# Decoder layer, cross-attention: the last slot of a pair of heads issues no value product, the first slot of the next pair issues two

## The reference

```python
q = (x @ Wq).reshape(B, S, 8, 64); k = (context @ Wk)...; v = (context @ Wv)...
attn = jnp.einsum('bhsd,bhld->bhsl', q, k) * 64 ** -0.5
attn = jax.nn.softmax(attn, axis=-1)
out = jnp.einsum('bhsl,bhld->bhsd', attn, v)
x = layernorm(x + out.reshape(B, S, 512) @ Wo + bo)
```

## Time and profile before

| | |
|---|---|
| median of 3 runs | 1456.46 us (1456.46 to 1459.16) |
| the profiled execution | 1461.65 us, its span 1459.9 us |
| mean granted TensorE clock | 0.906 |
| TensorE busy | 1227.4 us, 84% of the span |
| VectorE, ScalarE, GpSimd busy | 739.8, 579.5 and 683.9 us |
| the cross-attention's matmuls L1587 | 372.3 to 1089.7 us |

### The profile page before, as it was taken

One profiled execution on the slowest core, in us unless ns is written; L12 is line 12 of the kernel. 1 busy time (PEld: TensorE's weight loads), 2 busy tenths in 40 slices (PEclk: granted clock), 3 DMA queues, 4 the chain that ended last, 5 costly groups with the idle time before them and its releaser, 6 DMA issues.

```text
span 1459.9 us, 20289 instructions
## 1 busy us (share of the span) xinstructions
PE 1227.4 (84%) x6416; PEld 706.0 (48%) x6416; DVE 739.8 (51%) x1328; ACT 579.5 (40%) x999; POOL 683.9 (47%) x597
## 2 busy tenths in 40 slices
PE   4487787875899999999999999999994359999970
PEld 3255454543555555555545555555533336666640
DVE  6575858636335673456734667346613522222217
ACT  3365555642444554445544445444441012222210
POOL 0033333331357875578755877558782521111111
PEclk8688888975899999999999999999995579999995
DMA  5590000010000010000100000000004811111113
GB/s 176 177 303 16 1 1 0 0 46 23 0 1 1 1 46 1 1 1 1 46 2 1 1 1 24 0 1 1 1 1 138 293 56 44 42 46 45 45 51 136
DMA packets 33008, 64.66 MB, mean 44 GB/s; under 512 B 4222, under 2 KB 22399, under 8 KB 32641
## 3 DMA queue, kind: packets, MB, share of 16 engines
q1 hardware_dynamic: 23200, 32.41, 6.9%
q10 hardware_dynamic: 6304, 22.59, 4.9%
q0 software_dynamic: 3408, 8.43, 1.7%
HBM read 52.89 MB, written 28.34 MB: 56 GB/s over the span
## 4 chain that ended last, share of the span: by engine, by line
PE 68%; DVE 14%; issue 9%; ACT 4%; DMA 2%; POOL 1%; another core or an unknown queue 1%; ACTq 1%; SPq 0%; DVEq 0%; POOLq 0%
PE PS L1587 15%; PE PS L1598 11%; PE PS L1694 9%; PE PS L1515 9%; PE PS L1711 5%; PE PS L1528 3%; PE PS L1422 2%; PE PS L225 2%; DVE mxp L1173 2%; PE PS L1432 2%; PE PS L1411 2%; PE PS L226 2%; PE PS L227 2%; PE PS L1703 1%; PE PS L1568 1%
## 5 line engine op out<-in xcount | busy, mean ns | idle before, releaser
L609 POOL TENSOR_TENSOR acc<-acc,PX 128x1024 f32<-128x1024 f32 (+1 forms) x176 | 419.8, 2385 | 124.8 <-ACT PX L851 118.1
L851 ACT ACTIVATE PX<-PS 128x1024 f32<-128x1024 f32 (+1 forms) x208 | 213.3, 1025 | 266.5 <-PE PS L1587 262.3
L1173 DVE TENSOR_REDUCE mxp<-PS 128x2 f32<-128x804 f32 x256 | 241.6, 988 | 140.0 <-PE PS L1528 140.0
L1598 PE MATMUL PS<-PX,V 128*64 128x512 f32 (+1 forms) x832 | 223.3, 616 | 3.5 <-ACT O_raw L814 3.5
L551 POOL TENSOR_SCALAR_AFFINE_SELECT A<-A 128x128 f32<-128x128 f32 x256 | 89.1, 360 | 217.5 <-ACT A L752 214.0
L1694 PE MATMUL PS<-W,XBT 128*128 x312 | 148.8, 600 | 1.3 <-ACT XBT L907 1.3
L752 ACT ACTIVATE A<-PS 128x512 f32<-128x512 f32 (+3 forms) x256 | 99.4, 437 | 96.1 <-PE PS L1422 88.9
L670 POOL DMA_INDIRECT Y<-yb,goal_u x39 | 38.4, 985 | 201.0 <-DVE yb L1332 195.9
L1587 PEld LDWEIGHTS PS<-QH,KH 64*128 64x128 f32 (+1 forms) x416 | 38.3, 180 | 152.7 <-issue 89.5
L1422 PE MATMUL PS<-qT,kT 128*128 128x512 f32 (+3 forms) x256 | 87.4, 416 | 27.3 <-ACT A L752 22.0
L1587 PE MATMUL PS<-QH,KH 64*128 64x512 f32 (+1 forms) x416 | 104.0, 497 | 1.6 <-ACT MR L836 0.7
(11 more groups left out here) (261 smaller groups left out, 2068.9 us busy)
## 6 DMA issues: line engine op xcount, KB each, us to landing
W<-in_w SPq DMA_DIRECT2D x24, 512.0 KB
XB<-XG ACTq DMA_DIRECT2D x39, 129.0 KB, 2.1
yl<-Y SPq DMA_DIRECT2D x4, 1024.0 KB, 9.0
X<-in_x SPq DMA_DIRECT2D x1, 2048.0 KB, 12.1
out<-X SPq DMA_DIRECT2D x4, 512.0 KB, 2.9
xt_raw<-in_xt SPq DMA_DIRECT2D x3, 512.0 KB, 4.2
c_raw<-in_ctxt SPq DMA_DIRECT2D x6, 200.0 KB, 2.5
c_raw<-in_ctxt SPq DMA_DIRECT2D x12, 100.0 KB, 2.7
```

Of the source, the lines that this page charges most:

```text
L609: ins = pool.tensor_tensor(sums[0:r], sums[0:r], PX[0:r, (NL * p + t) % NP, :, :], ALU.add)
L851: act.activation(PX[0:r, u % NP, :, :], PS[0:r, score_buffer(u):score_buffer(u) + 2, :], ACT.Exp, scale=XD ** -0.5)\
L1173: dve.tensor_reduce(mxp[:, p % 2, :, v % NT, v // NT:v // NT + 1].rearrange("p a o -> p (a o)"), PS[:, k:k + 2, 0:BW], AX, ALU.max)\
L1598: mm = pe.matmul(PS[rows, 4, :], V[0:LROWS[j], j, P * p + XD * half:P * p + XD * half + XD], PX[0:LROWS[j], u % NP, half, :], start=(j == ...
```

## The change

TensorE's order of value products is changed at each boundary of two pairs. Before, the last slot (j = 12) of a pair issues the product of slot 11, and the first slot of the next pair that of slot 12. Now the last slot issues none, and the first slot of the next pair (or, from the fourth pair, of the next element) issues both, 11 and then 12. At the very end of the stage nothing moves: the products of slots 11 and 12 of the last pair stand behind the score products as before, only the first of them is now written behind the loop nest instead of in its last slot. The other slots, and the other engines, are as before. No wait is added or removed.

```diff
--- before.py
+++ after.py
@@ -1612,10 +1612,14 @@
                             scores_t(b + 1, 0)
                         for d, s in maxima(p, j, more) + early(p, j, first, more):
                             step(b + d, s)
-                        if u >= 1:
+                        if j == 0 and u >= 1:
+                            values_t(b, u - 2)
                             values_t(b, u - 1)
-                        elif not first:
+                        elif j == 0 and not first:
+                            values_t(b - 1, U - 2)
                             values_t(b - 1, U - 1)
+                        elif 1 <= j < NL - 1:
+                            values_t(b, u - 1)
                         for d, s in late(p, j, first, more):
                             step(b + d, s)
 
@@ -1626,6 +1630,7 @@
             with pe.Fori(1, B - 1) as b:
                 cross_attention(b, False, True)
             cross_attention(B - 1, False, False)
+            values_t(B - 1, U - 2)
             values_t(B - 1, U - 1)
             for s in EPILOGUE:
                 step(B - 1, s)
```

## The result

| | before | after |
|---|---|---|
| median of 22 runs each | 1458.62 us | 1454.03 us |
| lowest to highest | 1456.42 to 1462.46 us | 1448.82 to 1459.18 us |
| ratio of the medians, 95% interval | | 0.9966, 0.9953 to 0.9978 |
| the profiled execution, its span | 1461.65, 1459.9 us | 1454.91, 1453.2 us |
| first score product to the last totals ("stage") | 372.3 to 1097.1: 724.8 us | 369.5 to 1088.2: 718.7 us |

The change makes the kernel 0.34% faster: 4.6 us between the medians, where 5.0 us were forecast. The time itself, 1454.03, is 2.5 us above the forecast of 1451.5, mostly because the median of before over 22 runs is 2.2 us above that of the three runs from which the 5.0 were taken.

What follows compares the result with a forecast made beforehand. TensorE's own instruction stream was taken to bound the cross-attention stage. Boundary terms 3.06 + 0 + 1.22 + 0.71 = 5.0 us, taken off the median of 1456.46, gave 1451.5 us, range 1449.0 to 1456.6.

Steps and rivals of the forecast that it cites:

- Ordinary boundary: Nine pair boundaries without context preparation: same matmuls, fewer changes of kind, 0.19 from scores plus 0.15 from values, 0.34 us each.
- Rival 2: Neighbouring matmuls of one kind save nothing; only 1.5 us gained in all, median 1455.0 us; chance 10%.
- Nothing new waits there: At ordinary boundaries the reordered score, value and totals products meet no new wait on exponentials, QL or ACT's copies.
- O_raw boundaries: Pairs 2 to 3 of the first three elements: TensorE arrives 0.34 us earlier, waits that much longer; 0 us gained.
- Entry and exit of the loop: Two element crossings: the two value products side by side, the value projection's wait for QL gone; 0.61 us each.
- The way back: Taken branch of the element loop: less cover for its 3.43 us, but the value projection starts earlier; 0.7 us gained.
- The clock, zero net: Granted clock after TensorE's idle times: between 1.7 us gained and 5.1 lost, taken as zero.
- Rival 1: Longer waits for O_raw bring the clock down: one fall 1453.2, two 1454.9, three 1456.6 us; chance 28%.
- The sum: All boundary terms together: 3.06 + 0 + 1.22 + 0.71 = 5.0 us off the median of 1456.46 us.

Runs made afterwards that it cites:

- split_v: Against the changed kernel: at pair boundaries the product of slot 11 stands ahead of the query projection, that of slot 12 behind it; stage 722.7 us.
- one_slot_early: Against the changed kernel: slot 11 issues no value product, slot 12 issues those of 10 and 11, the next pair's first slot that of 12; stage 733.2 us.
- after_again: The changed kernel, unedited, traced a second time; stage 719.3 us.
- inner_only: Against the changed kernel: the product moves only at the twelve boundaries inside an element; element crossings and stage end as in the kernel before; stage 720.2 us.
- before_again: The kernel before, unedited, traced a second time; stage 723.2 us.
- before_context_later: Against the kernel before: ACT's casts of context chunks 2 and 3 come one slot later in pair 3; stage 725.2 us.
- slot1_too: Against the changed kernel: slot 1 of a pair also issues no value product and slot 2 issues two; stage 720.8 us.

## Why the prediction was right, point by point

- **Ordinary boundary, 0.34 us.** Right, to the hundredth: 5.87 to 5.53 us, S14 1.04 us behind S13, V V 1.87. At the last of the nine, where no Q stands, it is 0.32. split_v showed both parts, 0.19 and 0.15. Rival 2 (neighbours save nothing) is refuted.
- **Nothing new waits there.** Right. one_slot_early shows how near a wait was: with the gap one slot earlier TensorE waits 1.0 us a boundary.
- **O_raw boundaries, 0.** Nearly right: 0.0 to 0.2 us lost each. The idle time was to be 1.45 to 1.6 us and is 1.34 to 1.61 over the two traces of after, but in two pieces, since at these places QL is late too: ACT's cast QH stands behind the casts of the context. The prediction weighed T's wait for QL at the ordinary boundaries alone. It named DVE in the chain that makes O_raw late, but not that GpSimd's addition stretches the first of DVE's differences there; the 0 us did not hang on that.
- **Entry and exit of the loop, 0.61 each.** Right: 0.62, and the wait for QL is gone.
- **The way back, 0.71.** Right: 0.73 between the second traces and 0.83 between the first, with 1.11 us of idling where 1.2 was expected. The branch takes 3.31 to 3.73 us over the traces, so the size of this term scatters by some tenths. To go by the row of 3.43 us was right: without the cover of V11 the branch stands out by 1.11 us, and it did not grow (3.33 us in both traces of after).
- **The clock, zero net.** Rival 1 did not happen in the traces: after, after_again and inner_only show no fall between T1 and T15. The fall of the earlier trace rows went away, but it is absent from before_again as well. In other kernels falls came behind single waits of 1.26 us (before_context_later), 1.53 and 1.9 to 2.1; none behind 1.48 in slot1_too and 1.54 in one_slot_early. So a net of zero was in part luck: the rows on record could not tell which waits a fall follows, and the first trace of before had one where the second had none. The rival's premise also failed by the point above: no piece of idling at O_raw grew past 1.3 us.
- **The sum, 5.0.** Measured 4.6 between the medians; by the traces 4.3 from T1 to T15 and 0.34 for the first boundary, 4.6 too. The weak step was the base: three runs of before, with a median 2.2 us below that of 22.
- What I did not foresee concerns only the experiments: the gain at the O_raw boundaries is held by a second limit under the first, which the prediction had no need to know.

## What to carry to other kernels

Where the matmul stream is full, products of one kind side by side save 0.12 to 0.19 us here for each change of tiling that vanishes; first ask which engine's answer the moved product was covering. A wait that is taken away uncovers the next one, so look three or four steps on before costing it. When an operation of VectorE over SBUF takes several times its usual length, look at what GpSimd is doing beside it.

## What the runs showed of the hardware that was not expected

- A VectorE copy of 128x256 takes 0.28 us alone and 2.12 us beside a GpSimd addition that was there first; a difference of 64x399 takes 0.57, 1.53 beside a multiplication and 2.79 beside an addition. With a GpSimd write of zeros beside it, it takes 0.57. Reductions from PSUM (0.93 to 1.00 us each) and reciprocals (1.70 to 1.76) do not change.
- The taken branch of the cross-attention's loop takes 3.3 to 3.7 us of TensorE's queue, the one not taken 0.08 us. With S13, V11 and W as cover it stood out by 0.2 to 0.5 us, without V11 by 1.1 to 1.4. It is not the price of every taken branch: that of the first stage's loop, L1501 in the same traces, takes 0.24 us. In the trace of after some 2240 instructions of TensorE's queue lie between the two branches of the one loop, some 820 between those of the other; whether their size is the cause was not tried.
- The granted clock fell to its lower level (1.2 GHz) behind one wait of 1.26 us and did not behind one of 1.54: the length of the idle time alone does not tell.
